# Scan operands of an attention-and-state-space kernel: rows on every second partition, and one load in place of two

## What is computed

```
def step(h, inputs):
    ad, bd, xt, ct = inputs
    h = jnp.clip(h * ad[:, :, None] + bd[:, :, None] * xt[:, None, :], -10.0, 10.0)
    yt = jnp.einsum('bd,bdh->bh', ct, h)
    return (h, yt)
_, ys = jax.lax.scan(step, h0, (Ad, Bd, xn, Cm))        # 256 steps
y = ys.transpose(1, 0, 2) + D * xn
return y * jax.nn.silu(gate) @ W_out.T
```

## Time and profile before

| what | us |
|---|---|
| median of 3 runs | 548.18 (547.77 to 550.46) |
| the profiled execution | 549.22 |
| its span, first to last instruction | 547.4 |
| scan: first DVE step starts | 336.31 |
| scan: last DVE step starts | 536.78 |
| DVE busy | 431.0 (79% of the span) |
| PE busy | 473.7 (87%) |
| granted TensorE clock, mean | 0.971 |

### The profile page before, as it was taken

The page is one execution under the profiler, slowest core; times in us unless marked ns, Lnnn a source line. Parts: engine busy times, 40 slices in busy tenths (PEclk is TensorE's granted clock), DMA queues, the critical chain, the costliest instruction groups (busy, mean ns, idle before and its releaser), DMA issues.

```text
span 547.4 us, 8477 instructions
## 1 busy us (share of the span) xinstructions
PE 473.7 (87%) x3014; PEld 282.7 (52%) x3034; DVE 431.0 (79%) x754; ACT 254.9 (47%) x510; POOL 174.5 (32%) x196
## 2 busy tenths in 40 slices
PE   1938898999999989888999787799899999998996
PEld 1834656767676666567887553133333333333333
DVE  6836464767857776749997975999999999999993
ACT  2340577767577646778777666243321111111111
POOL 6344213113031100000730003588784334333332
PEclk9977799999999999999999997999999999999999
DMA  8866065644645520110065376675446433333310
GB/s 330 341 176 170 1 144 128 156 114 115 160 99 152 135 78 2 39 38 3 0 243 192 119 230 136 225 260 189 156 135 129 144 122 112 108 102 103 103 38 19
DMA packets 44741, 71.80 MB, mean 131 GB/s; under 512 B 18937, under 2 KB 33657, under 8 KB 41580
## 3 DMA queue, kind: packets, MB, share of 16 engines
q1 hardware_dynamic: 37420, 67.07, 41.8%
q0 software_dynamic: 528, 3.55, 1.7%
q10 hardware_dynamic: 6752, 0.65, 0.9%
HBM read 41.88 MB, written 23.02 MB: 119 GB/s over the span
## 4 chain that ended last, share of the span: by engine, by line
PE 53%; DVE 31%; ACT 6%; DMA 4%; issue 3%; SPq 1%; POOL 0%; ACTq 0%; DVEq 0%
DVE win L1773 11%; PE bank L982 7%; PE bank L1411 6%; PE bank L1035 5%; PE bank L1371 5%; PE bank L1382 5%; DVE z L1773 5%; PE bank L1005 5%; PE bank L1020 4%; PE bank L1084 3%; PE bank L1062 3%; DVE acc L1561 3%; DVE zlast L1773 2%; DVE lnb_rep L1773 2%; PE bank L1209 2%
## 5 line engine op out<-in xcount | busy, mean ns | idle before, releaser
L1583 DVE TENSOR_REDUCE mx<-bank 128x2 f32<-128x512 f32 x128 | 82.3, 687 | 65.5 <-PE bank L1005 65.4
L1371 PE MATMUL bank<-xst,bst 128*128 128x512 bf16 x238 | 78.3, 394 | 21.8 <-DVE win L1773 8.8
L706 ACT ACTIVATE ex<-bank 128x512 f32<-128x512 f32 x128 | 70.9, 600 | 36.7 <-PE bank L1020 36.7
L1773 DVE CUSTOM_DVE_ANT_0 win<-win,bank,hi 128x512 f32<-128x512 f32 x96 | 71.8, 748 | 3.4
L1371 PEld LDWEIGHTS bank<-xst,bst 128*128 128x128 bf16 x256 | 24.8, 98 | 72.8 <-DVE win L1773 31.6
L474 POOL TENSOR_TENSOR qk<-qk,part 128x512 f32<-128x512 f32 x16 | 19.0, 1190 | 121.5 <-ACT part L631 121.5
L1005 PE MATMUL bank<-kst,qst 127*128 127x256 bf16 x256 | 48.1, 280 | 6.2 <-DVE mx L1583 5.6
L982 PE MATMUL bank<-xnT,w 128*128 128x256 f32 x192 | 50.4, 418 | 0.9 <-ACT vp L651 0.8
L1020 PE MATMUL bank<-qst,kst 128*128 128x256 bf16 x256 | 46.1, 273 | 5.4 <-ACT ex L706 3.2
L576 POOL TENSOR_TENSOR yg<-yT,gateT 128x128 f32<-128x128 f32 x60 | 29.2, 522 | 59.2 <-ACT yT L915 59.2
L907 ACT ACTIVATE ytk<-bank,ybias 128x512 f32<-128x512 f32 x15 | 10.3, 687 | 72.9 <-PE bank L1382 72.9
(11 more groups left out here) (202 smaller groups left out, 907.9 us busy)
## 6 DMA issues: line engine op xcount, KB each, us to landing
qk_d<-part SPq DMA_DIRECT2D x60, 96.0 KB, 2.4
xs_d<-xpart SPq DMA_DIRECT2D x15, 384.0 KB, 4.2
xst<-xs_d SPq DMA_DIRECT2D x15, 384.0 KB
xn_d<-xc SPq DMA_DIRECT2D x16, 256.0 KB, 3.2
xtk<-xn_d SPq DMA_DIRECT2D x64, 64.0 KB
xst<-xs_d SPq DMA_DIRECT2D x15, 256.0 KB
bd_d<-zeros POOLq DMA_DIRECT2D x1, 3468.0 KB, 12.1
qst<-qk_d SPq DMA_DIRECT2D x8, 384.0 KB, 3.9
```

The lines of the kernel that those rows point to most:

```text
L706: nc.scalar.activation(ex[:, n // 4, n % 4, :], bank[6 + n % 2][:, :], ACT.Exp, scale=SCALE)\
L1371: mm(bank[t % 4][:, :], bst[:, slot, t % RS, :], xst[slot][:, t % RS, :], start=True, stop=True)\
L1583: v.tensor_reduce(mx[:, :, STACKED[n]:STACKED[n] + 1], bank[4 + n % 2][:, :].rearrange("p (t k) -> p t k", t=HALVES), AX.X, ALU.max)\
L1773: v._custom_dve(bass.dve_ops.TENSOR_ADD_SAT, out=zst[t % ZR], in0=zst[(t - 1) % ZR], in1=bank[t % 4][:, :], s0=hi[:, t:t + 1], s1=0.0).the ...
```

## The change

x's rows move to every second partition in one series: 24 rows on 0, 2, ..., 46, then (after three partitions 48, 50, 52 that stay 1.0) 16 rows on 54, ..., 84 and 8 rows on 86, ..., 100. b's 51 rows then lie on 0, 2, ..., 100 without a break and are contiguous in DRAM too, so that one transfer of 51 rows takes the place of those of 27 and 24. The number of rows, the bytes and the matmuls are as they were. PE waits for 16 counts of a b load's semaphore in place of 32.

```diff
-X_ROWS = ((0, 3), (33, 2), (97, 1))
+X_ROWS = ((0, 3), (54, 2), (86, 1))
...
-                    sp.dma_start(xst[i % 2][at:min(at + 4 * run * B, P):4, lo:hi, :],
+                    sp.dma_start(xst[i % 2][at:at + 2 * run * B:2, lo:hi, :],
...
-                for at, row, count in ((0, 0, 27), (33, 27, 24)):
-                    rows = bd_d[row * BP:(row + count) * BP].rearrange("(r t c) -> r t c", r=count, c=P)
-                    sp.dma_start(bst[at:min(at + 4 * count, P):4, i % 2, lo:hi, :],
-                                 rows[:, i * RS + lo:i * RS + hi, :]).then_inc(s[name], 16)
+                rows = bd_d[0:51 * BP].rearrange("(r t c) -> r t c", r=51, c=P)
+                sp.dma_start(bst[0:102:2, i % 2, lo:hi, :], rows[:, i * RS + lo:i * RS + hi, :]).then_inc(s[name], 16)
...
-                        pe.wait_ge(s["ld_bf"], 32)
+                        pe.wait_ge(s["ld_bf"], 16)
...
-                            pe.wait_ge(s[f"ld_b{slot}"], 32 * (i // 2 + 1))
+                            pe.wait_ge(s[f"ld_b{slot}"], 16 * (i // 2 + 1))
```

## The result

The changed kernel takes 553.48 us (median of 4 runs, 553.30 to 556.41), the kernel before beside it 548.27 us (4 runs, 547.77 to 550.46): a ratio of 1.0112, 95% interval 1.0071 to 1.0153, so 5.2 us or 1.1% slower. That is half a microsecond above the range, and the chance of "slower" was put at 0.27. The profiled execution took 553.3 us, with a span of 551.5 us.

The account below looks back on a forecast made before the run. The scan, where DVE hardly idles at 0.78 us a step, was taken to bound the kernel, with b's first load exposed. Terms of 0.4 + 0.4 + 0.7 = +1.5 us took the median from 548.18 to 549.7; range 547.6 to 553.0.

Parts of the forecast that it names:

- term 1: Scan's start: b's first load, on three engines, lands later; +0.4 us taken, bounds -0.77 to +1.7.
- term 2: First rounds: b's backlog on three engines delays round 2 (step 32) by +0.4 us, bounds 0 to +1.5; round 1 unaffected.
- Three engines: b's load: 51 rows run on three DMA engines, 17 rows each, adding 1.9 us to a whole round's b.
- rival C: x's loads: rows on every second partition slow x, 0.6 to 1.2 us a round; 552.5 to 554.5, likeliest 553; chance 0.22.
- Term 3: Round 7, issued late: b's 1.9 us delays step 112 by +0.7 us, bounds 0 to +1.5.
- The later rounds: Rounds other than the start, 2 and 7 swallow b's added 1.9 us; no idle in rounds 8 to 15.
- Rival B: 51 rows spread over 16 engines; the start gains 0.77 us, nothing else changes: 547.4 us; chance 0.06.
- Rival A: Rounds 2 and 7 find gaps in the queues, only the first load's delay is left: 548.6 us; chance 0.15.

Follow-up runs that it names:

- e2: Kernel before, old places kept, b's rows blocked in DRAM and brought by three loads on three engines: 553.45 us beside 548.67, ratio 1.0089.
- e3: Changed kernel, but b brought by two loads of 48 rows (16 engines) and 3 rows: 548.66 us beside 548.67, ratio 0.9991.
- e4: Changed kernel, but b's single load has 52 rows, the last of zeros (13 engines): 548.72 us beside 548.67, ratio 0.9988.
- e1: Changed kernel with the new places, but b again brought by two loads of 27 and 24 rows: 549.57 us beside 548.67, ratio 1.0017.
- e7: Changed kernel, but b brought by two loads in rounds 0, 1, 2 and 7, one in the 12 others: 549.01 us beside 548.42, ratio 1.0012.
- e5: Changed kernel, but the second group's xtk (skip-row) loads issued behind round 2's operands: 551.65 us beside 548.42, ratio 1.0067.
- e8: Changed kernel, but b brought by two loads in round 7 alone: 553.18 us beside 548.42, ratio 1.0100.
- e9: Changed kernel, but one b load of 52 rows and the second group's xtk loads behind round 2's operands: 547.81 us beside 549.29, ratio 0.9979.
- e6: Changed kernel, but rows on adjacent partitions 0 to 50 and b by two loads of 27 and 24 rows: 568.03 us beside 548.42, ratio 1.0381.
- e10: Changed kernel, but b's single load has 53 rows, two of them zeros (one engine): 622.46 us beside 549.29, ratio 1.1318.

## Why the prediction was wrong, point by point

**The sum.** By the profiles, predicted and measured: first load 0.4 and 1.7; step 8 nothing and -0.25; round 1 nothing and 1.2; round 2 0.4 and 1.6; round 7 0.7 and 1.05. That is 1.5 us against 5.2. Of the 3.7 us that are missing, 1.3 are term 1's and 2.1 term 2's. The working also gave bounds of up to 1.7, 1.5 and 1.5 for the terms, 4.7 together or 552.9 us, yet took 551.5 as the forecast's upper end, as if the terms could not all be high at once. They have one cause in common, and terms 1 and 2 came out at their bounds or past them.

**Three engines: right.** 63 small packets and 18.9% are what it said. It is also what the loss hangs on: e2 has the loss without the new places, e3 and e4 have the new places without the loss.

**Term 1, the first load: mis-sized, +1.7 in place of +0.4.** The upper bound was worked out for the case that ACT's queue of 32-byte packets halves b's rate on its engines, and I took the value near the lower end, because the earlier trace rows had many packets of SP's queue moving. Those were spread over nine and twelve engines. What decides is how long the busiest engine needs, and that one now has 17 packets to place among ACT's, not 5. ACT's queue held half of the engines' time there (331:336, after), as its share shows, and in 332.9:335.2 there are 1520 - 1480 = 40 packets of 2 KB, the size of b's rows in round 0:

```profile
q10 hardware_dynamic: 4384, 0.14, 50.0%
```
```profile
DMA packets 1552, 0.44 MB, mean 191 GB/s; under 512 B 1431, under 2 KB 1480, under 8 KB 1520
```

40 packets on three engines in 2.3 us are 0.17 us each, against 0.09 where nothing else runs. So the rate was halved, as the upper bound had it. Single starts scatter: kernels that are the same up to the first step differ by 0.6 or 0.7 us (e1 7.69 and e7 7.09; after 8.89, e5 8.28 and e8 8.98). By groups, one load of 51 rows has 8.3 to 9.0 us and one of 52 rows 6.2 and 6.5, with the same issues: three engines cost about 2.3 us there, near the 2.5 of the upper bound.

**Term 2, rounds 1 and 2: the step that failed.** "Short of step 16 at 349.31" was wrong: round 1 was put at nothing and cost about 0.9 net (1.17 at step 16, less the 0.25 saved at step 8), and round 2 cost 1.59 in place of 0.4. The working had b's own 1.9 us only. In the changed kernel b of round 1 is there at 349.55 in place of 346.15, 3.4 later: 1.9 for b's rows, 0.9 for x ahead of it, whose slowing I had put into rival C alone, and 0.6 because SP reaches the round later. SP's timeline after, to be held against the earlier trace rows:

```profile
340.06 2.04 SPq L368 DMA_DIRECT2D xst<-xs_d  x3
342.14 0.68 SPq L375 DMA_DIRECT2D bst<-bd_d  x1
```

SP waits for the store of line 357 before it issues round 1, and that store stands in the queue behind both halves of b's round 0. It took 6.1 us from issue to landing in place of 2.9 (first the kernel before, then after):

```profile
xs_d<-xpart SPq DMA_DIRECT2D x1, 336.0 KB, 2.9
```
```profile
xs_d<-xpart SPq DMA_DIRECT2D x1, 336.0 KB, 6.1
```

Thirteen of the sixteen engines' parts had landed by 336.96, the other three at 338.93 to 339.87, behind b's second half (337.82 to 338.75): three engines held it up, and what stood in their queue came in order. The first step is 0.6 us later as well, so against DVE the round's b is 2.8 us late. A stall then costs more than itself. The stretches of after about step 16:

```profile
345.00:349.60 4.60, 2.14 (x11) 0.41 (x11) 4.42 (x6) 0.00 (x0) 0.72 (x1) 1.00 0.65 236
349.60:352.00 2.40, 2.36 (x8) 0.64 (x12) 1.20 (x3) 0.00 (x0) 0.00 (x0) 0.52 0.50 149
```

PE's idle is followed by a granted clock of 0.52, and its first two products take 1.02 us (the chain above) in place of 0.64. From landing to step it is 1.23 us in place of 0.8. Round 2 fits an addition: 3.4 from round 1, again 1.9 and 0.9, so 6.2 us, and its b is there at 364.10 in place of 357.89 (6.2), though its x was issued 0.7 us earlier than before (350.17, 350.89). The split into 1.9 and 0.9 is the arithmetic of these two traces; e1, above, puts more of it on the places. The prediction had 3.8 of backlog and an idle of 0.4; the trace has 1.59. So the two terms "the rows on three engines" and "x is slower" were right each for itself, but were put into two cases that exclude each other. Where the margin holds one of them and not both they add, and the one that comes last spends it.

**Term 3, round 7: nearly right.** Expected was an idle of 0.7 (0 to 1.5), the profile has 1.05. From x's issue at 418.43 to b's landing at 427.77 it is 9.3 us, against 7.0 before (415.54 to 422.50): 2.4 more in place of 1.9, and the rest, 0.5, would be the slower x, less than the 0.9 of a later round. It stands on the profile of after; the times of e8 don't settle it.

**The later rounds: right.** No idle at 48, 64 and 80, and by e7 one slow load in each of twelve rounds costs nothing that can be told.

**Rival C** named 552.5 to 554.5 with 553 likeliest, which is where the time fell, and that is luck in part: its mechanism alone is e1, +0.9 us (-0.5 to 2.3), where it was priced at 3 to 5 on top of the forecast's terms. Its 2 to 3 us of backlog are there (3.1 at round 2 in e1), but the round's margin takes them up; they count only once b is late too. **Rival B** is refuted by the 63 packets; the starts of e4 and e9 (6.50 and 6.23) show that its 0.8 us would have come with 13 engines. **Rival A** falls with rounds 1, 2 and 7.

**Open.** How the 5.2 us of the changed kernel divide between engines (4.8 in e2, which has two issues more) and places (0.9 in e1) can't be told closer than about 1.5 us either way, half the width of their intervals, and their sum need not be what they cost together. How much of e5's gain is the shorter queue and how much SP's earlier issue was not separated. Whether round 1 is late varies from run to run, and what decides it was not found.

## What to carry to other kernels

Before two loads are joined, work out on how many DMA engines the joined one runs (here the largest divisor up to 16 of its row count: 52 rows 13 engines, 51 rows 3, 53 rows 1), and if the count is bad, pad it or cut off a remainder; the count of small packets in a stretch tells it in one look. Price a slower transfer at the rounds with the least margin, and there add all that changes, the transfers ahead of it and the issue that waits for a store included, since a margin is spent only once. Keep rows that a load writes apart across the partitions; adjacent ones cost twice the transfer time here.

## What the runs showed of the hardware

- **SP's time for a DMA issue depends on how the partitions are spaced.** All instructions on x's line (368) and b's (376), ns least/median/most: first the two of e1 (every second partition), then the two of e6 (adjacent).

```profile
L368 SPq DMA_DIRECT2D xst<-xs_d x51: 527/618/873, 326.8 to 509.3; - x51
```
```profile
L376 SPq DMA_DIRECT2D bst<-bd_d x34: 715/724/736, 329.1 to 510.7; - x34
```
```profile
L368 SPq DMA_DIRECT2D xst<-xs_d x51: 290/318/756, 328.1 to 527.2; - x51
```
```profile
L376 SPq DMA_DIRECT2D bst<-bd_d x34: 282/312/389, 329.6 to 527.8; - x34
```

  The same rows and bytes are issued in 0.31 us in place of 0.72. In this kernel the slower transfer costs far more than that gives back.
- **A joined issue is not dearer than a part.** 51 rows are issued in 680 ns, 27 or 24 rows in 728.
- **A PE stall of about 2 us can bring a second one.** The granted clock fell to 0.50 behind it for some 2 us, in e4 with a second DVE idle of 1.41 us. In e10 ten of the eleven stalls were followed by a second DVE idle of 1.3 to 1.9 us, one by 0.16. Behind the 1.9-us stall of round 2 in the changed kernel the clock stayed at 1.00 (362 to 368), so it doesn't do so each time.
- **A load on few engines holds up a later transfer on all of them.** The store of line 357 landed on thirteen engines 3.2 us after its issue and on the last three after 5.2 to 6.2, behind b's rows.
